# First attention of a gated cross-attention stack: VectorE's part written out batch by batch

## The reference

```python
Q = (x_text @ Wq).reshape(Bb, Tt, H, DH)        # 16 x 256 x 4 x 32
K = (x_vision @ Wk).reshape(Bb, Gg, H, DH)      # 16 x 1601 x 4 x 32
scores = jnp.einsum('bthd,bghd->bhtg', Q, K) / np.sqrt(DH)
topv, topi = jax.lax.top_k(scores, K_TOP)       # 32 of 1601
probs = jax.nn.softmax(topv, axis=-1)
attn = jnp.zeros_like(scores).at[bi, hi, ti, topi].set(probs)
attn_mean = attn.mean(axis=1)
c_t = jnp.einsum('btg,bgd->btd', attn_mean, x_vision @ Wv)
```

## Time and profile before

| what | us |
|---|---|
| median of three runs | 3156.57 |
| lowest and highest of them | 3145.81, 3169.88 |
| the profiled execution, its own time | 3151.31 |
| its span, first to last instruction | 3149.8 |
| first attention, DVE's first to its last batch | 249.3 to 1322.9 of the span |

### The profile page before, as it was taken

How to read it: one execution, slowest core, us unless ns; L and a number is a source line. 1 busy time by engine, 2 the same in 40 slices (tenths; PEclk the granted TensorE clock), 3 DMA queues, 4 the chain that set the end, 5 groups by cost and what they waited for, 6 DMA issues and landing times. The chain is left out here.

```text
span 3149.8 us, 68581 instructions
## 1 busy us (share of the span) xinstructions
PE 2576.0 (82%) x19758; PEld 1301.7 (41%) x19758; DVE 2353.5 (75%) x8066; ACT 2083.1 (66%) x3430; POOL 1263.5 (40%) x1597
## 2 busy tenths in 40 slices
PE   7757888888788888667786599999999999999278
PEld 5544555555555555534422133333333333333245
DVE  8607989898988888736555999898989889991422
ACT  4537879888888888714321088787878778889022
POOL 1315778777777777713200503222222222100432
PEclk8878989889988888888897599999999999999589
DMA  6540000000000000081331133332323233220221
GB/s 197 175 160 14 13 12 14 20 14 12 12 12 14 20 14 12 5 269 56 58 112 36 64 62 99 92 89 86 98 83 87 84 94 99 76 50 2 86 72 45
DMA packets 159444, 205.97 MB, mean 65 GB/s; under 512 B 74511, under 2 KB 127053, under 8 KB 159081
## 3 DMA queue, kind: packets, MB, share of 16 engines
q1 hardware_dynamic: 148732, 161.85, 19.1%
q0 software_dynamic: 10352, 39.92, 3.7%
HBM read 135.21 MB, written 66.62 MB: 64 GB/s over the span
## 5 line engine op out<-in xcount | busy, mean ns | idle before, releaser
L2146 ACT ACTIVATE pb<-sps 128x512 f32<-128x512 f32 (+1 forms) x1664 | 894.1, 597 | 283.9 <-PE sps L2088 270.1
L2169 DVE TENSOR_REDUCE mx<-wps 128x2 f32<-128x802 f32 x1024 | 954.2, 989 | 96.1 <-PE wps L2061 80.7
L1081 DVE MAX8 cand<-sc 128x8 f32<-128x46 f32 (+1 forms) x4480 | 585.4, 193 | 172.7 <-ACT sc L960 91.9
L846 PE MATMUL scores<-ctxT,qT 97*128 97x512 f32 (+1 forms) x1024 | 471.1, 612 | 106.7 <-ACT sc L960 92.8
L2103 PE MATMUL ops<-pb,va 128*9 128x256 f32 x6656 | 530.2, 390 | 9.4 <-ACT ot L2152 8.5
L846 PEld LDWEIGHTS scores<-ctxT,qT 97*128 97x128 f32 x1024 | 216.1, 221 | 366.0 <-issue 253.1
L1945 POOL COPY va<-XX 128x128 f32<-128x128 f32 (+1 forms) x208 | 49.9, 293 | 710.6 <-PE ops L2103 702.7
L729 POOL TENSOR_TENSOR prf<-sc,prf 128x1601 f32<-128x1601 f32 x64 | 230.0, 3594 | 91.1 <-ACT prf L967 91.1
L2061 PE MATMUL wps<-FO,Y 56*128 56x401 bf16 x1024 | 196.8, 368 | 49.4 <-DVE mx L2169 34.5
L729 POOL TENSOR_TENSOR prs<-sc,prs 128x1601 f32<-128x1601 f32 x64 | 230.6, 3603 | 5.4 <-POOL xn L703 3.6
L821 PE MATMUL misc<-diag,prs 128*128 128x128 f32 (+1 forms) x1664 | 224.9, 289 | 6.6 <-issue 6.6
(11 more groups left out here) (410 smaller groups left out, 4087.9 us busy)
## 6 DMA issues: line engine op xcount, KB each, us to landing
FO<-keys SPq DMA_DIRECT2D x392, 50.0 KB
XX<-keys SPq DMA_DIRECT2D x392, 50.0 KB
keys<-kpb POOLq DMA_DIRECT2D x42, 400.2 KB, 3.5
toep<-kernpad SPq DMA_DIRECT2D x8, 2048.0 KB, 15.2
values<-s_vs SPq DMA_DIRECT2D x16, 832.0 KB, 6.0
XX<-values SPq DMA_DIRECT2D x16, 832.0 KB, 4.5
keysf<-s_kf SPq DMA_DIRECT2D x16, 800.5 KB, 3.8
Y<-queries SPq DMA_DIRECT2D x784, 8.0 KB
```

The source lines that it names most:

```text
L846: ins = t.matmul(scores[:, c:c + n], q, ctxT[par][0:C + 1, c:c + n], start=True, stop=True)
L1081: st.add(v.max(cand[s % 2][:, n, :], sc[s % 4][:, c:c + w]))
L2146: nc.scalar.activation(pb[(UNITS * g + u) % 8][0:rows_, :, :], sps[(UNITS * g + u) % SB][0:rows_, :, :], ACT.Exp).then_inc(p_ready, 1)
L2169: v.tensor_reduce(mx4[:, q, h:h + 2, c], both, AX.X, ALU.max).then_inc(work_read, 1)
```

## The change

DVE no longer hands its `step` to `walk`. A plain loop of the program that builds the kernel calls it 16 times, so that the instructions of all 16 batches stand one behind the other and the batch number is a constant in each. `step` itself is the same; of its arguments DVE's version does not use `par` and `visit`. PE, ACT, POOL and SP still use `walk`.

```diff
@@ -1139,7 +1139,9 @@
                 v.scalar_tensor_tensor(out=pr[s][:, :], in0=pr[s - 1][:, :], scalar=r, in1=pr[s][:, :],
                                        op0=ALU.mult, op1=ALU.add).then_inc(pair_done, 1)
 
-            walk(dve, step)
+
+            for b in range(B):
+                step(b, b % 2, None, b == 0, b == B - 1)
             settle(NS - 1, NS * B - 1)
             add_pair(NS - 1, NS * B - 1, st.link, iter(()))
```

## The result

The changed kernel takes 3116.19 us (median of four runs, 3112.14 to 3128.59) against 3153.89 of the kernel before: a ratio of 0.9881, 95% interval 0.9833 to 0.9929. Two later comparisons of the same pair gave 0.9843 (0.9803 to 0.9883) and 0.9884 (0.9852 to 0.9916). The forecast was 3129 us, in a range of 3108 to 3154. The sum behind it was 25.0 us off; measured are 37.7.

What follows compares the result with a forecast made beforehand. VectorE was taken to bound the first attention, busy 60.5 of about 66 us a batch. Terms 18.0 + 1.6 + 5.4 = 25.0 us, from 3154 to 3129 us; range 3108 to 3154.

Steps and rivals of the forecast that it cites:

- The stall lies on the path and nothing covers it: Head of batches after a jump back: VectorE's idle gap lengthens ScalarE's wait at line 967 by 3.07 us, nearly the whole stall.
- The term of 18.0 us: First attention, VectorE's loop: six jumps back go, worth 3.0 us each; bounds 0 and 20.9 us.
- The registers at 1.6 us: VectorE's wait for scores, line 1095: register arithmetic goes, some 40 operations of 0.04 us; bounds 0 and 3.9 us.
- The lower clock behind a jump, 5.4 us: TensorE after line 854's wait: six batches lose 0.9 us each as the clock stays higher; bounds 0 and 8.3 us.
- The sum's base: Whole kernel: 3154 us, the middle between bases from the profiled execution, 3151.31 us, and the median run, 3156.57 us.
- The first rival: First attention: ScalarE or TensorE takes up what VectorE gives back, leaving 7.0 us gain, 3147 us; chance 0.15.
- The second: Ends of slots, line 1074: forward jumps in fresh code stall 3.0 us, one a batch, giving 3171 us; chance 0.05.
- The third: First attention: TensorE's clock stays up, every batch comes to 64.70 us, 44 us gain, 3110 us; chance 0.15.
- the third term: TensorE's lower clock behind the six jumps back: 5.4 us gained, bounds 0 and 8.3 us.

Runs made afterwards that it cites:

- The one pair of kernels made to measure it: Against the changed kernel: VectorE's loop with one jump back, register arithmetic kept, 0.9929; and one stall added at batch 8, no registers, 0.9914.
- the last kernel: Changed kernel with all engines written out batch by batch and six unused multiplications in each of TensorE's two long waits per batch: 3084.75 us, ratio 0.9773.
- the one before it: Changed kernel with all engines written out batch by batch, not VectorE alone, without filling: 3118.82 us, ratio 0.9885.
- The filled kernels: Changed kernel with six unused multiplications in each of two TensorE waits per batch, 0.9876; the same with all engines written out, 0.9773.
- The filled stall: Changed kernel with six added VectorE stalls and ten unused multiplications in TensorE's wait ahead of the count of slot 0: 3143.84 us, ratio 0.9978.

## Why the prediction was right, point by point

**The stall lies on the path and nothing covers it.** Right, and shown: the gaps, ACT's waits and the length of the six batches went as written, and six stalls made by another instruction bring most of the time back. The term of 18.0 us is what the head of the batch gave: the six gaps are 1.5 us together instead of 20.3, so 18.8 of the six batches' 28.8 us. That the engine stands for a fetch of code fits the packet on q14 in every such gap; it was read from the trace, and no kernel varied it by itself.

**The registers at 1.6 us.** The gap at a batch's head is 0.25 us where it was 0.35 without a jump, so a tenth of a microsecond a place where the term counted 0.04. With the term's 40 places that is 4 us (an estimate), just above its upper bound. The one pair of kernels made to measure it points to more and did not separate it from nothing; open.

**The lower clock behind a jump, 5.4 us, bounds 0 and 8.3.** Either this term was too small, or the registers are in what is left for it: the six batches lost 28.8 us, 18.8 by the gaps; 10.0 are left, above the upper bound. The kernel with six added stalls has PE's wait and no register arithmetic; there the stalls themselves come to 18 us of its 24 in the stage and leave 6, near the 5.4, but one profile is uncertain by 7. The bound came from the eight batches without a jump, and took those at 65.88 us as what the six would become; they became 65.5. The clock in the six was 0.83 to 0.90 in the rows shown and is 0.90 to 0.92 now. That the lower clock makes a batch longer is what the last kernel shows, which differs from the one before it by the filling (1044.7 to 1013.8 us), on the slot whose rows stand above. That PE's 4.10 us wait at line 854 is what lowers it, as I had it, is not shown: with that wait cut to 1.88 us the clock stayed at 0.77.

**The sum's base.** By profiles the change is worth 29.6 us (five of them), by medians of the runs 38, 43 and 37. The 8 us between are not accounted for; profiled executions of the changed kernel lay some 5 us above the median of its runs (3120.9 on the mean of three, 3115.6 the median of all fourteen).

**The first rival**, that ACT or PE takes up the stall, had a little in it: DVE's waits at line 1134 grew by 3.6 us in the first pair (24.5 and 25.1 us in the two profiles before, 27.0 to 28.1 in the three after), of the 18 that it would have needed. **The second**, stalls at forward jumps in fresh code, did not come: no VectorE gap near 3 us stands at a batch's head, and the stage is shorter. Some gaps at the ends of slots are as long as 3.7 us, but the kernel before has them too; away from the batches' heads 5 and 10 gaps are longer than 2.5 us in its two profiles, 3, 3 and 6 in the three of the changed kernel. Batch 0 has seven of the branches of line 1074, not eight as the argument against this rival says; that changes nothing in it. **The third**, the clock up everywhere and every batch at 64.7 us, did not come by the change (65.7 us on the mean of the 14 batches); the last kernel comes to 62.4 on the mean, with one batch of 70.2.

**The size.** By the medians the sum missed by 12.7 us. Some 8 of these are the difference between profiles and medians. By the profiles the miss is 4.6 (29.6 against 25.0), no more than the third term fell short by (10.0 against 5.4). Of that, 2.9 us is the third of the difference between the two kinds of batch that I left out, since the last of the eight was long as well. The measured 3116 us lies below the 3121 to 3136 that the terms' own bounds give. It lies in the stated range because that was widened for the spread of the runs and for a part of the third rival, which did not come; so far the range held by its allowance and not by the sum.

## What to carry to other kernels

A jump back in the busiest engine's loop is to be priced by the gap at the loop's head and by what the next engine waits there; if that engine has finished its work in both cases, as ACT had, the whole gap counts. Not every jump back has a gap: look for it in the trace, loop by loop. The jumps of ACT, POOL and PE left no idle time, and writing these loops out, which takes away their registers as well, showed in the time only beside the filling (1044.6 us for the stage with the filling alone, 1013.8 with both). And where the fastest engine on the path is paced by another's clock, look at PE's short waits: filling two of them with unused work was worth 35 us together with written-out code, and nothing that could be told from chance without it.

## What the runs showed that I had not expected

Two edits that gave nothing measurable each (ratios 0.9876 and 0.9885, the changed kernel 0.9843 to 0.9884) gave 34.6 us together. The batches of the first attention come in steps, about 64.0, 65.7 and 67.4 us in the changed kernel, that go with PE's granted clock of 0.95, 0.90 and 0.87; the same program runs through different series of these steps from one execution to the next, and this is most of the 14 us by which three profiles of one kernel differ. The Trainium skill, "TensorE: Matmul & The Clock Gate", Part 1: The HAM clock gate, lets activity release the clock; the filled kernels agree with 0.92 and 0.93 over the stage. The filled stall does not show it: 0.77 with 11.21 us of work in 15, as with 9.04.
